# Draining the adapter product's accumulators two at a time between the passes of a top-k search, and four passes sooner

## The reference

```python
xn = layernorm(x)
# gated MLP with a sparse gate, I = 11008
s = silu(xn @ w_gate.T)
idx = top_k(-abs(s), I // 2)          # the smaller half of each token's row
s = s with s[idx] = 0
mlp = (s * (xn @ w_up.T)) @ w_down.T
# base product plus eight small adapters, O = 4096
base = xn @ W_base.T + b_base
gate = softmax(xn @ W_gate.T); thr = sigmoid(xn @ W_thr + b_thr) * 0.125
w = relu(gate - thr), divided by its sum
moe = einsum('ner,ne,eor->no', xn @ A_w.T, w, B_w) * 2
x = x + mlp + (base + moe)
```

## Time and profile before

| | us |
|---|---|
| two runs | 5870.26 and 6103.4 |
| their median | 5986.83 |
| the profiled execution | 5881.75 |
| span of its slowest core (core 6), from the first to the last instruction | 5880.2 |
| spans of its eight cores | 5836.7 to 5880.2 |

### The profile page before, as it was taken

The page is one execution under the profiler, slowest core; times in us unless marked ns, Lnnn a source line. Parts: engine busy times, 40 slices in busy tenths (PEclk is TensorE's granted clock), DMA queues, the critical chain, the costliest instruction groups (busy, mean ns, idle before and its releaser), DMA issues.

```text
span 5880.2 us, 51349 instructions; the slowest of 8 cores (5836.7 to 5880.2 us)
## 1 busy us (share of the span) xinstructions
PE 4418.2 (75%) x20408; PEld 1986.8 (34%) x20408; DVE 1319.6 (22%) x1928; ACT 1213.5 (21%) x1522; POOL 546.6 (9%) x640
## 2 busy tenths in 40 slices
PE   5999944640699998787859998446406999987877
PEld 2444411210244453333324444112102444533333
DVE  2000065488300000000020000654883000000000
ACT  2000064476200040000020001544761000400000
POOL 0111100000011101010101111000000111010100
PEclk9999977765899979898969999777658999798989
DMA  6999946550699959999959999355406999599998
GB/s 128 146 147 146 122 58 86 84 74 0 94 144 144 144 76 149 145 147 147 153 120 148 146 146 127 56 84 87 67 0 99 144 144 144 76 149 144 146 149 138
DMA packets 669369, 683.02 MB, mean 116 GB/s; under 512 B 31184, under 2 KB 651728, under 8 KB 668112
## 3 DMA queue, kind: packets, MB, share of 16 engines
q0 software_dynamic: 631120, 612.61, 74.9%
q1 hardware_dynamic: 38016, 67.13, 3.6%
HBM read 1267.07 MB, written 25.17 MB: 220 GB/s over the span
## 4 chain that ended last, share of the span: by engine, by line
PE 68%; ACT 9%; DVE 8%; issue 7%; DMA 7%; SPq 1%; DVEq 0%; ACTq 0%; POOL 0%; POOLq 0%
PE q L507 20%; PE q L370 20%; PE q L470 19%; ACT sc L592 8%; PE q L428 6%; DMA xs<-x 3%; PE pt L486 2%; DVE st L755 2%; DMA ffn_scr<-ffst 2%; DVE S L813 1%; DMA ovr<-x 1%; DVE lns L651 1%; ACT S L541 0%; DVE S L805 0%; DVE st L787 0%
## 5 line engine op out<-in xcount | busy, mean ns | idle before, releaser
L470 PE MATMUL q<-wst,xT 128*128 128x512 f16 (+1 forms) x5632 | 1227.4, 377 | 582.4 <-DVE S L813 532.8
L507 PE MATMUL q<-wst,S 128*128 128x512 f16 x4128 | 1151.0, 388 | 224.1 <-DVE ovr L832 224.1
L370 PE MATMUL q<-wst,xT 128*128 128x512 f16 (+1 forms) x5632 | 1221.3, 375 | 27.2 <-ACT S L541 9.4
L470 PEld LDWEIGHTS q<-wst,xT 128*128 128x128 f16 x5632 | 549.4, 98 | 1260.8 <-issue 653.1
L592 ACT ACTIVATE sc<-ovr,st 128x6400 f16<-128x6400 f16 x144 | 810.5, 5628 | 267.2 <-DVE st L792 227.7
L428 PE MATMUL q<-wst,xT 128*128 128x512 f16 x2048 | 490.2, 402 | 400.0 <-ACT ffst L577 259.6
L370 PEld LDWEIGHTS q<-wst,xT 128*128 128x128 f16 x5632 | 548.9, 98 | 699.4 <-issue 87.3
L767 DVE TENSOR_SCALAR_CACHE_REDUCE sc<-ovr,st 128x4608 f16<-128x4608 f16 x144 | 721.7, 5012 | 65.5 <-ACT sc L592 47.9
L507 PEld LDWEIGHTS q<-wst,S 128*128 128x128 f16 x4128 | 410.5, 99 | 740.6 <-issue 275.5
L507 PE MATMUL q<-wst,sc 128*128 128x512 f16 x1376 | 532.6, 387 | 20.0 <-DVE ovr L832 17.2
L428 PEld LDWEIGHTS q<-wst,xT 128*128 128x128 f16 x2048 | 207.3, 102 | 683.1 <-issue 468.0
(11 more groups left out here) (79 smaller groups left out, 1206.1 us busy)
## 6 DMA issues: line engine op xcount, KB each, us to landing
wst<-wgT POOLq DMA_DIRECT2D x168, 1024.0 KB, 9.9
wst<-wuT POOLq DMA_DIRECT2D x168, 1024.0 KB, 10.5
wst<-wdT POOLq DMA_DIRECT2D x160, 1024.0 KB, 11.7
wst<-wbT POOLq DMA_DIRECT2D x64, 1024.0 KB, 12.3
ovr<-x SPq DMA_DIRECT2D x8, 2048.0 KB, 7.9
xs<-x SPq DMA_DIRECT2D x64, 256.0 KB, 5.7
y<-ovr SPq DMA_DIRECT2D x64, 256.0 KB, 5.6
wst<-wdT POOLq DMA_DIRECT2D x16, 768.0 KB, 9.1
```

What stands on the lines that cost most here:

```text
L370: mm = mark(tensor.matmul(quad[m][:, 0:wl], xT[:, k * 512 + m * 128: k * 512 + (m + 1) * 128], wst[:, slot * SLOTB + kk * wl: slot * SLOTB ...
L470: mm = mark(tensor.matmul(quad[m][:, 0:wl], xT[:, k * 512 + m * 128: k * 512 + (m + 1) * 128], wst[:, slot * SLOTB + kk * wl: slot * SLOTB ...
L507: mm = mark(tensor.matmul(quad[m][:, 0:512], lhs, wst[:, slot * SLOTB + kk * 512: slot * SLOTB + (kk + 1) * 512], start=(k == 0), stop=(k ...
```

## The change

One place is changed, the part of ScalarE's order that stands behind each pass. Behind pass 4 and later passes of tile 0 (before: pass 8 and later), and behind each pass of the other tiles, up to two drains are made where one was made. The drains themselves, their waits, their order and their number stay as they are.

```diff
@@ -597,8 +597,10 @@
                             ).then_inc(aCR, 1)
                         if m == 0 and it < NT:
                             drain_hwt(pend_hwt.pop(0))
-                        elif pend_ffn and (m >= 1 or it >= 8):
+                        elif pend_ffn and (m >= 1 or it >= 4):
                             drain_ffn()
+                            if pend_ffn:
+                                drain_ffn()
                 while pend_ffn:
                     drain_ffn()
                 for m in range(NT):
```

## The result

| | kernel before | changed kernel |
|---|---|---|
| median of all runs, us | 5913.56 (39 runs) | 5900.49 (40 runs) |
| ratio to the kernel before | | 1.0036, 95% interval 1.0021 to 1.0051 |
| profiled execution, spans of the eight cores, us | 5836.7 to 5880.2 | 5871.7 to 5888.8 |

The changed kernel is slower by 0.36%, some 21 us at a level of 5870 us. The sign came out, the size did not: the loss is less than a third of the sum.

What follows compares the result with a forecast made beforehand. ScalarE and VectorE were taken to bound the search, with ScalarE stalling for TensorE's base product. Per half, 172.7 us of losses minus 136.8 gave 35.9; 72 us on 5881.75 made 5954 us, range 5890 to 6070 us.

Steps and rivals of the forecast that it cites:

- the sum: Search losses per half, 172.7 us minus the present 136.8, give 35.9 us; 72 us for both halves, carried to the end.
- forecast 1095: Base product on TensorE: the eighth result comes near 1095 us instead of 1219 us, which buys nothing.
- Six long stalls per half and a seventh that nearly hides: ScalarE's search: rounds 1 to 6 still stall it; round 7 hides behind a tile change, except 2.1 us.
- Fewer passes in each round: Search: a 43.3 us round holds two passes, 14.9 us, losing 28.4 us per round against 22.8 before.
- The second drain hidden in VectorE's gap: ScalarE beside a pass: the second drain's 0.56 us fits the 1.25 us left in its gap and costs nothing.
- The store waits at the third and fourth drain: ScalarE's drains: with two buffers, waiting for stores puts the third at t + 10.1, the fourth about t + 11.3.
- Weights, not drains, start the round: TensorE's round start: drains done at about 11.9 us, weights there at 12.0 us after the previous round's first drain starts.
- The rival of late third and fourth items: Base product runs: later weight items come late every round, 6 us per run; 6026 us, slower by over 2%, chance 0.15.
- t + 12.0: TensorE's next base round starts 12.0 us after t, the start of the previous round's first drain, when its weights land.
- 43.3 us: Cycle of a base round after the change: 12.0 us until it starts plus 31.3 us until its result can be drained.
- twice 35.9: Net extra search time of 35.9 us in each half, 72 us for both.

Runs made afterwards that it cites:

- a_stores4: Changed kernel with four buffers instead of two for the stored base product, so no drain waits for a store; ratio that of the changed kernel within 0.2%.
- b_delay: Kernel before with four more counting passes on VectorE alone behind each half's search, everything after it 20 us later; ratio to the kernel before 1.0060.
- a_weights: Changed kernel with bias and adapter weights in buffers outside the ring, so a round's first weight items are asked for earlier; ratio to the kernel before 1.0006.

## Why the prediction was wrong in size

**Right.** ScalarE and VectorE set the end of the search and TensorE doesn't: its restart behind L815 came later although the base product ended 127 us sooner (the eighth round's first drain at 1091.96 us instead of 1219.12 us, forecast 1095). Six long stalls per half and a seventh that nearly hides (6.28 us idle). Fewer passes in each round: two. The second drain hidden in VectorE's gap. The store waits at the third and fourth drain, 30.3 us in all. Weights, not drains, start the round, but by little: on core 7 the fourth drain ends at t + 10.3 and the run begins at t + 10.7 (forecast 11.9 and 12.0), and on cores 4 and 6 some rounds began with the drain; without the waits for stores the weights still hold the round at 40.9 us (`a_stores4`). The rival of late third and fourth items is refuted: a run of 128 matmuls on core 7 took 29.1 to 30.7 us.

**Mis-sized: the start of a round, "t + 12.0".** Its mechanism held (the weights end last, by little), but the changed kernel measures t + 8.6 to 9.4 on core 6 and t + 9.4 to 11.7 on core 7 from the second drained round of each half on. The size was read on core 6 of the kernel before, and it is a different one on other cores. In the kernel before the list of waits has for core 4 and then for core 5:

```profile
PE q L428 <- DMA wst<-wbT: 101.0, 12, 9.8
```

```profile
PE q L428 <- DMA wst<-wbT: 141.5, 12, 13.2
```

Cores 0, 3 and 4 wait 8.4 to 9.3 us for a round's first item in the mean of the twelve, their neighbours 1, 2 and 5 11.4 to 12.1 us. Cores 6 and 7 issue within 1 us of each other for most of half 1 and wait 11.7 and 10.3 us. Before the change this didn't show in any time, as the fourth drain came at 21 us. After it, it does. ScalarE's timeline of core 6 of the changed kernel, and below it TensorE's:

```profile
871.83 1.07 ACT L577 CAST ffst<-q 128x512 f16<-128x512 f32 x2 [26.18 <-PE q L449]
...
912.54 1.07 ACT L577 CAST ffst<-q 128x512 f16<-128x512 f32 x2 [26.21 <-PE q L449]
```

```profile
880.93 29.97 PE L428 MATMUL q<-wst,xT 128*128 128x512 f16 x128 [8.81 <-ACT ffst L577]
...
921.81 3.57 PE L428 MATMUL q<-wst,xT 128*128 128x512 f16 x8 [8.98 <-DMA wst<-wbT]
```

It has rounds of 40.7 us, core 7 has 42.4 us (838.04 to 1050.25 over five); the forecast was 43.3 us for all. The slower neighbour falls behind by 1 to 2 us a round, and by the table of items above a core further behind waits less: its own first item comes 11.7 us behind the first drain ahead of the fifth round, and 10.1 us ahead of the last. In half 2 the cores of a pair enter the search 10 to 12.5 us apart, and there the rounds of core 7 take 41.5 us in the mean, against 42.5 us in half 1. So the term fed back on itself, and the search cost 25.6 and 19.2 us instead of twice 35.9: 27 of the 51 us that are missing.

**Failed: "the sum", which put everything behind the search at nothing.** The forecast carried a delay of the search one to one to the end and gives no reason for it. But the down product has a wait of its own on transfers, 100 us a half in gaps of 14 us, and it got 24.9 us shorter; that is the rest of what is missing. No line of that stage is changed. That a mere shift doesn't do it is shown by `b_delay`. That the search had pushed the cores of a pair 15 us apart and that this shortened the stage is not shown in the same way: it rests on the 56 pairs, on the gaps within one kernel, and on how two neighbours' requests hold each other up in the base product. The reads of `x` are not the way it works, or not the only one, since the pairs with reads four deep still differ by 12 us. Which transfers it goes through, and which shared part of the two cores' way to memory slows them, stays open.

One reading in the forecast goes further than its source. In the Trainium skill, DMA: Bandwidth & Descriptors, section Anatomy of one DMA, the fit is given for transfers that GpSimd issues; the weight loads are such, the stores of SyncE are not.

## What to carry to other kernels

Where an engine's order mixes its own loop with drains that wait for another engine, count the stalls and the loop steps that lie between them: draining faster than the producer can refill only packs fewer steps between equal or longer stalls, while a spacing that gives the producer its time (31 us, here five passes) removes them (4.6% here). A wait that is hidden today must be sized on every core, not on the slowest, before it is taken for what will bind tomorrow; when cores begin to differ in time, look at the next stage that waits for memory, even if it lies a millisecond behind the change.

## What the runs showed of the hardware that was not expected

Two neighbouring cores that do the same at the same time slow each other's transfers, and it is the second to ask that waits: the first 1 MB weight item of a base round landed 9.1 us after its issue on a core that asked over 1 us ahead of its neighbour, 13.1 us on one that asked 1 to 4 us behind, and 12.8 us where both asked within 1 us. A down product with reads two deep took 734.7 us at a distance below 6 us and 721.5 us above 9.5 us. The Trainium skill, Trainium Kernel Development and Optimization, section NeuronCore Architecture, lists main storage per pair of cores. This case's traces agree in so far as the order of the requests counts only between the two cores of a pair. And a store of 128 KB lands later when it is issued beside two weight items: 4.5 to 9.6 us after its issue on core 7 of the changed kernel (median 7.1), 1.7 to 5.6 us on core 7 of `a_weights` (median 2.7), where the items are sent earlier and no drain waited for a store.
